# Graph network on one core: in the first edge stage the scatters wait for two copies at a time, the second following the first directly

## The chip, the cores and the metric

One Trainium2 chip, one of its cores. The time is the device time of one execution in microseconds (us); of several runs the median counts. A core has five engines that run side by side and meet by semaphores: TensorE (PE in the rows; PEld are its weight loads), VectorE (DVE), ScalarE (ACT), GpSimd (POOL) and SyncE (SP), which issues most DMAs. All DMAs are carried out by the core's 16 DMA engines. Indirect DMAs, whose rows are chosen by a list of indices, are issued by GpSimd.

## The reference, cut to what matters

A two-layer graph network on 12500 nodes of 160 features and 200000 edges, sorted by destination (`dst`), with random sources (`src`). The stage at hand is the message part of layer 0. Each edge takes the features of its `dst` node, mixes them with the edge's four attributes, and adds the message to its `src` node:

```
xj = node_features[col]                        # col = dst
m0 = s @ Wm_ss * dist * INV8 + einsum('eui,ei->eu', v, r_vec) @ Wm_vv * (...)
m1 = (s @ Wm_sv)[:, :, None] * r_vec[:, None, :] * INV8 + einsum('eui,uw->ewi', v, Wm_vs) * dist[:, :, None] * ...
msg = concatenate([m0, m1.reshape(e, 96)], axis=-1)
agg = segment_sum(msg, row, num_segments=n)    # row = src
```

The products with the weights are done per node in a stage before and stored in a table `T0`, so the edge stage gathers, scales and adds up. The sum over `u` of the vector parts is left as 32 partial sums, so a message has 192 numbers (`MSG0`). Layer 1, an attention layer, and the node updates follow in later stages.

## The kernel before, in words

The function `layer0_edges` (L328) runs through the edges in tiles of 128 (`R`), four tiles (`GT`) to a step, 392 steps in all, 8 steps (`STEPS`) to a pass of the loop (`passes`, L321). In a step, for each of its four tiles:

- SP loads the rows of `T0` that the tile needs (`e_win`, L389 and L390), three steps ahead. Once in four steps it loads also `e_local` (L377), `e_row` (L373, the tile's source nodes repeated over 128 partitions, 1024 KB), `e_at` (L369), and the data of a part of layer 1 that runs in this stage beside the edges (`r_xT` L682 in, `H` L690 out; class `Radial`).
- TensorE spreads the rows to the edges (L584), VectorE and ScalarE form the messages `u` (L476 to L486, L625). The edges of a tile may share a source node, and an accumulating scatter must not name a row twice; so TensorE multiplies the messages with the matrix `q` of equal sources (L597), which gives every edge the total of its node in this tile, and ranks.
- ScalarE copies the four tiles' totals from PSUM into one of four buffers (`e_total`, `evacuate`, L638). Ahead of that it waits until the scatters of the step four back, which read the same buffer, have landed.
- VectorE works out in `places` (L525 to L540) where each row goes: the first edge of a node in a tile to the node's row, all others to a dump row (`e_place`).
- GpSimd issues four indirect DMAs that add the rows to HBM (`sums`, L447), one per tile. Tile c of each step goes to its own copy of the sums, `sums[c]`; the four copies are added up in the next stage (`node_update0`). Since an accumulating DMA reads the sum and writes it later, the scatter into copy c must wait until the scatter of the step before into the same copy has landed. For this there are semaphores `added[p][c]`, by the parity p of the step and by the copy, which each scatter raises by 16.

The wait stands not at the scatter but at a tiny instruction ahead of it: `settle` (class `Settle`, L119) waits for its own last result and adds two zeros in one element (`e_pool_cell`, L129), and the scatter follows it in order on GpSimd. In a step's body, for c = 0 to 3: at c = 0 the waits for the buffer and the places (`total_ready`, `placed`); then the wait for `added[1 - p][c]`; then `settle`; then the scatter of copy c. `gate` (L113) is a wait that always holds.

Of the kernel before, what the change touches and what calls it, by code (L numbers as in the profile page):

```python
# [77 lines left out]
class Mem:  # L78
# [15 lines left out]
    def sem(self, name):  # L94
        self.sems.append(self.nc.alloc_semaphore(name))
        return self.sems[-1]
# [16 lines left out]
def gate(eng, k):  # L113


    eng.wait_ge(k["ready"], 4)
# [204 lines left out]
def passes(eng, body):  # L321
    body(0)
    with eng.Fori(1, PASSES - 1) as t:
        body(t)
    body(PASSES - 1)


def layer0_edges(nc, m, k, ps, W, T0, index, rows_src, LR, baseI, iota, attr, sums, es, H):  # L328
# [4 lines left out]
    with own:  # L333
# [15 lines left out]
        added = [[sem(f"e0_added{p}{c}") for c in range(GT)] for p in range(2)]  # L349
# [10 lines left out]
        settle = Settle(mm, k, "e0_pool")  # L360
# [4 lines left out]
        with nc.Block() as block:  # L365
# [66 lines left out]
            @block.gpsimd  # L432
            def _(pool):
                def body(t):
                    for r in range(STEPS):
                        i, p = At(t, r), r % 2
                        for c in range(GT):
                            if c == 0:
                                gate(pool, k)
                                pool.wait_ge(total_ready, i.n(1, 1))  # L440
                                gate(pool, k)
                                pool.wait_ge(placed, i.n(1, 1))
                            if not i.before(1):
                                gate(pool, k)
                                pool.wait_ge(added[1 - p][c], i.uses(64, 16 * ((r + 1) // 2)))
                            settle(pool, i.n(4, c))
                            pool.indirect_dma_start(sums[c], bass.IndirectOffsetOnAxis(ap=place[:, r % 4, c:c + 1], axis=0),  # L447
                                                    total[:, r % 4, c, 0:MSG0], None, compute_op=ALU.add
                                                    ).then_inc(added[p][c], 16)
                passes(pool, body)  # L450
                for p in range(2):
                    for c in range(GT):
                        pool.wait_ge(added[p][c], 16 * (SB // 2))
# [2518 lines left out]
```

## Time and profile before

| | us |
|---|---|
| median of 3 runs | 10577.76 |
| lowest, highest | 10567.25, 10608.22 |
| profiled execution | 10625.38 |
| its span | 10623.6 |

| engine | busy us | share of the span |
|---|---|---|
| PE | 8642.2 | 81% |
| DVE | 8012.2 | 75% |
| POOL | 7869.8 | 74% |
| PEld | 5524.9 | 52% |
| ACT | 4337.2 | 41% |

The shares are means over stages that are bound by different things. The first edge stage runs from about 487 to 3530 us of the span, so the views are to be read for this stretch. A row of the groups by line names the line, the engine, the operation, what it writes and reads, its count, the busy time in us and the mean time of one in ns, then the engine's idle time just before these instructions and what ended it. A row of the timeline has the start in us, the duration in us, engine, line and operation, and in brackets the idle time just before it. Of a DMA that GpSimd issues the row shows the time that GpSimd is busy with it, not the transfer. "issue" means that the engine waited for nothing that the profile shows.

### The profile page before, as it was taken

The numbers are of one execution on the slowest core, as the hardware profiler recorded it, in microseconds if no ns is written. First come the engines' busy times: TensorE is split into PE (matmuls) and PEld (weight loads), VectorE is DVE, ScalarE is ACT, GpSimd is POOL, SyncE is SP. The second block draws the span as 40 slices with busy tenths as digits, with TensorE's granted clock in tenths as the row PEclk, the third lists the DMA queues.
The fourth block names the chain that finished last, engine by engine and source line by source line (L and its number), as shares of the span: only waits on it lengthen the run. The fifth ranks groups of instructions, "written<-read, shape, count | busy, mean of one in ns | idle before, by whom it ended". The sixth has DMA issues, their size and how long they took to land. (4 is left out here: it accounts for less than half of the span.)

```text
span 10623.6 us, 176663 instructions
## 1 busy us (share of the span) xinstructions
PE 8642.2 (81%) x35512; PEld 5524.9 (52%) x35512; DVE 8012.2 (75%) x15399; ACT 4337.2 (41%) x7700; POOL 7869.8 (74%) x7782
## 2 busy tenths in 40 slices
PE   0888888888888799999996788777787878787588
PEld 0444444444444232222224777777777777777333
DVE  3277777777777588788886888888888888888565
ACT  0276666666666211111112333333333333333255
POOL 4488888888888777777775777777777777777332
PEclk9599999999999799999997989999899989899699
DMA  5588888888888999999993444444444444444222
GB/s 205 172 168 169 163 168 169 163 167 165 167 170 161 179 221 222 220 220 223 218 223 98 134 135 137 134 134 134 134 136 134 134 135 137 134 134 134 72 76 59
DMA packets 1202910, 1661.71 MB, mean 156 GB/s; under 512 B 215166, under 2 KB 814537, under 8 KB 1172553
## 3 DMA queue, kind: packets, MB, share of 16 engines
q1 hardware_dynamic: 806993, 1199.16, 42.2%
q0 software_dynamic: 395520, 458.93, 23.6%
q14 instruction: 353, 2.89, 0.1%
q8 instruction: 44, 0.72, 0.0%
HBM read 1483.21 MB, written 443.97 MB: 181 GB/s over the span
## 5 line engine op out<-in xcount | busy, mean ns | idle before, releaser
L447 POOL DMA_INDIRECT sums<-e_total,e_place x1568 | 2495.0, 1591 | 389.2 <-issue 223.0
L1847 POOL DMA_INDIRECT e_rows<-TD,e_at x1568 | 1613.6, 1029 | 477.6 <-issue 477.0
L1847 POOL DMA_INDIRECT e_rows<-TS,e_at x1568 | 1581.0, 1008 | 417.5 <-issue 330.5
L584 PE MATMUL ps<-e_win,e_pick 128*128 128x448 f32 x3136 | 1331.9, 570 | 165.2 <-DVE e_u L481 125.2
L2004 PE MATMUL ps<-w_r,e_h 128*128 128x224 f32 x3136 | 870.1, 432 | 518.4 <-DVE e_d L1889 470.5
L2108 ACT ACTIVATE e_dT<-ps 128x512 f32<-128x512 f32 x1176 | 671.7, 596 | 1185.7 <-PE ps L2016 1145.5
L584 PEld LDWEIGHTS ps<-e_win,e_pick 128*128 128x128 f32 x3136 | 614.7, 201 | 917.9 <-issue 833.1
L1098 POOL TENSOR_TENSOR n_zv<-n_zv,n_ast 128x1536 f32<-128x1536 f32 x200 | 730.8, 3654 | 467.6 <-DMA n_zv<-in_x_columns 456.9
L129 POOL TENSOR_TENSOR e_pool_cell<-zeros 1x1 f32<-1x1 f32 x1568 | 939.4, 599 | 87.5 <-DVE e_place L540 59.1
L2004 PEld LDWEIGHTS ps<-w_r,e_h 128*128 128x128 f32 x3136 | 675.8, 227 | 593.3 <-DVE e_d L1889 485.5
L2040 PE MATMUL ps<-w_lb,e_dT 128*128 128x192 f32 x3136 | 836.3, 348 | 4.6 <-issue 3.8
L1278 PE MATMUL ps<-n_z,w_uss 128*64 128x512 f32 x1600 | 745.1, 609 | 24.5 <-DVE n_z L1121 23.9
L2016 PE MATMUL ps<-ident,e_d 128*128 128x128 f32 x4704 | 743.2, 302 | 6.6 <-issue 4.2
L747 DVE SCALAR_TENSOR_TENSOR r_y<-ps,w_rb,r_rstd 128x512 f32<-128x512 f32 x394 | 295.5, 750 | 586.5 <-issue 516.2
L1102 POOL TENSOR_TENSOR n_zv<-n_zv 128x512 f32<-128x512 f32 x400 | 695.0, 1737 | 36.9 <-POOL n_zv L1102 0.4
L2016 PEld LDWEIGHTS ps<-ident,e_d 128*128 128x128 f32 x4704 | 661.7, 160 | 47.6 <-issue 7.9
L2028 PE MATMUL ps<-e_val,e_q 128*128 128x168 f32 x3136 | 642.0, 329 | 53.2 <-ACT e_tot L2119 19.1
L2041 PE MATMUL ps<-w_la,e_dT 128*128 128x160 f32 x3136 | 681.8, 299 | 0.0
L716 PE MATMUL ps<-r_sq,w_avg 128*128 128x512 f32 x788 | 446.9, 651 | 277.7 <-issue 277.7
L597 PEld LDWEIGHTS ps<-e_u,e_q 128*128 128x128 f32 x3136 | 541.7, 192 | 187.9 <-issue 187.9
L597 PE MATMUL ps<-e_u,e_q 128*128 128x194 f32 x3136 | 586.3, 330 | 0.0
L1859 DVE TENSOR_TENSOR e_m<-e_rows 128x640 f32<-128x640 f32 x392 | 321.7, 821 | 341.5 <-DMA e_rows<-TD,e_at 192.8
(433 smaller groups left out, 19205.2 us busy)
## 6 DMA issues: line engine op xcount, KB each, us to landing
e_win<-T SPq DMA_DIRECT2D x1568, 168.0 KB
n_z<-in_x_columns SPq DMA_DIRECT2D x400, 512.0 KB
n_zv<-in_x_columns SPq DMA_DIRECT2D x800, 192.0 KB
TOT<-e_tot SPq DMA_DIRECT2D x392, 352.0 KB
e_row<-in_src_rows SPq DMA_DIRECT2D x98, 1024.0 KB
e_row<-in_dst_rows SPq DMA_DIRECT2D x98, 1024.0 KB
e_win<-T SPq DMA_DIRECT2D x1568, 56.0 KB
e_local<-LR SPq DMA_DIRECT2D x98, 512.0 KB
```

The source lines that it names most:

```text
L129: pool.tensor_tensor(self.cell[:], z, z, ALU.add).then_inc(self.done, 1)
L447: pool.indirect_dma_start(sums[c], bass.IndirectOffsetOnAxis(ap=place[:, r % 4, c:c + 1], axis=0), total[:, r % 4, c, 0:MSG0], None, compu ...
L584: pe.matmul(g[:, c, :], pick[:, p, R * c:R * c + R], win[:, s, c, :], start=True, stop=True).then_inc(spread, 1)
L597: last = pe.matmul(out[:, c, :], q[:, p, c, :], u[:, p, c, :], start=True, stop=True)
L1098: pool.tensor_tensor(zv[:, b], zv[:, b], ast[:, g.p], ALU.mult).then_inc(zv_ready, 1)
L1102: pool.tensor_tensor(zv[:, b, 0], zv[:, b, 0], zv[:, b, i], ALU.add).then_inc(zv_ready, 1)
L1278: last = pe.matmul(ps[0:S, U0, :], W["uss"][:, 4 * s + j, :], z[:, s % 4, j, :], start=False, stop=False)
L1847: pool.indirect_dma_start(rows[:, p, x, c, :], None, table, bass.IndirectOffsetOnAxis(ap=at[:, gp, x, col:col + 1], axis=0)).then_inc(rows ...
L2004: last = pe.matmul(w4[:, c, 0:224], hh[:, p, R * c:R * c + R], W["r3"][:], start=True, stop=True)
L2016: last = pe.transpose(ps[:, bank(i, j), R * c:R * c + R], d[:, p, c, j, :], I[0:R, 0:R])
L2040: pe.matmul(head(c)[:, :, 0:24], dT[:, 1, e], W["lb"][:].rearrange("u h x -> u (h x)"), start=True, stop=False)
L2041: pe.matmul(head(c)[:, :, 0:20], dT[:, 0, e], W["la"][:].rearrange("u h x -> u (h x)"), start=False, stop=True)
```

## The change

The four scatters of a step form two pairs. Ahead of c = 0 GpSimd waits for the landings of the step before into copies 0 and 1, then there is one `settle`, and the scatters of copies 0 and 1 follow one another with nothing between; the same for copies 2 and 3. So there are two `settle` a step where there were four, and the scatters of copies 1 and 3 have their wait one scatter earlier. What is transferred stays the same.

```
-                            if not i.before(1):
-                                gate(pool, k)
-                                pool.wait_ge(added[1 - p][c], i.uses(64, 16 * ((r + 1) // 2)))
-                            settle(pool, i.n(4, c))
+                            if c % 2 == 0:
+                                for also in range(c, c + 2):
+                                    if not i.before(1):
+                                        gate(pool, k)
+                                        pool.wait_ge(added[1 - p][also], i.uses(64, 16 * ((r + 1) // 2)))
+                                settle(pool, i.n(2, c // 2))
                             pool.indirect_dma_start(sums[c], bass.IndirectOffsetOnAxis(ap=place[:, r % 4, c:c + 1], axis=0),
                                                     total[:, r % 4, c, 0:MSG0], None, compute_op=ALU.add
                                                     ).then_inc(added[p][c], 16)
```

## Rows read from the trace of the kernel before

**Rows 1.** Busy us (and instructions) per engine of one stretch, clock, DMA share, GB/s.

```profile
core 0: us, PE busy (x) PEld busy (x) DVE busy (x) ACT busy (x) POOL busy (x), PEclk, DMA share, GB/s
2000.00:2300.00 300.00, 254.32 (x775) 139.45 (x775) 214.08 (x485) 201.39 (x333) 257.82 (x312) 0.97 0.83 168
```

**Rows 2.** Groups by line, GpSimd, 480 to 3560 us.

```profile
L447 POOL DMA_INDIRECT sums<-e_total,e_place x1568 | 2495.0, 1591 | 389.2 <-issue 223.0 <-DMA sums<-e_total,e_place 152.1 <-POOL e_pool_cell L129 14.0
...
L129 POOL TENSOR_TENSOR e_pool_cell<-zeros 1x1 f32<-1x1 f32 x1568 | 939.4, 599 | 87.5 <-DVE e_place L540 59.1 <-DMA sums<-e_total,e_place 18.0 <-issue 10.1
```

**Rows 3.** Timeline of GpSimd: a step with e_row and the next one's start.

```profile
2008.14 2.04 POOL L447 DMA_INDIRECT sums<-e_total,e_place  x1 [0.24 <-DMA sums<-e_total,e_place]
...
2010.48 1.55 POOL L447 DMA_INDIRECT sums<-e_total,e_place  x1 [0.24 <-issue]
2011.49 0.61 POOL L129 TENSOR_TENSOR e_pool_cell<-zeros 1x1 f32<-1x1 f32 x1
2012.34 1.55 POOL L447 DMA_INDIRECT sums<-e_total,e_place  x1 [0.24 <-issue]
...
2014.20 1.55 POOL L447 DMA_INDIRECT sums<-e_total,e_place  x1 [0.24 <-issue]
2015.63 0.19 POOL L129 TENSOR_TENSOR e_pool_cell<-zeros 1x1 f32<-1x1 f32 x1
2016.28 1.55 POOL L447 DMA_INDIRECT sums<-e_total,e_place  x1 [0.46 <-DMA sums<-e_total,e_place]
```

**Rows 4.** Waits, 480 to 3560 us: waiting line, releaser: us in total, times, longest.

```profile
ACT e_total L638 <- DMA sums<-e_total,e_place: 368.0, 258, 3.3
...
POOL e_pool_cell L129 <- DMA sums<-e_total,e_place: 18.0, 22, 2.0
```

**Rows 5.** Timeline of ScalarE: its copies into the buffers (three of them).

```profile
2018.20 0.82 ACT L638 ACTIVATE e_total<-ps 128x776 f32<-128x776 f32 x1 [1.49 <-DMA sums<-e_total,e_place]
...
2035.17 0.82 ACT L638 ACTIVATE e_total<-ps 128x776 f32<-128x776 f32 x1 [1.04 <-DMA sums<-e_total,e_place]
...
2049.68 0.82 ACT L638 ACTIVATE e_total<-ps 128x776 f32<-128x776 f32 x1 [0.63 <-PE ps L597]
```

**Rows 6.** Timeline of GpSimd: plain scatters of an earlier stage, directly following.

```profile
300.18 0.96 POOL L833 DMA_INDIRECT T<-n_out,place_rank  x1 [1.31 <-DVE n_out L822]
301.44 0.96 POOL L833 DMA_INDIRECT T<-n_out,place_rank  x1 [0.30 <-issue]
```

**Rows 7.** Timeline of GpSimd: gathers of the second edge stage.

```profile
6008.48 0.95 POOL L1847 DMA_INDIRECT e_rows<-TD,e_at  x1 [0.30 <-issue]
6009.73 0.94 POOL L1847 DMA_INDIRECT e_rows<-TD,e_at  x1 [0.30 <-issue]
6010.68 0.18 POOL L129 TENSOR_TENSOR e_gather_cell<-zeros 1x1 f32<-1x1 f32 x1
6011.02 1.24 POOL L1847 DMA_INDIRECT e_rows<-TS,e_at  x1
```

**Rows 8.** Timeline of GpSimd: the stage's last scatter.

```profile
3521.40 1.55 POOL L447 DMA_INDIRECT sums<-e_total,e_place  x1 [0.24 <-DMA sums<-e_total,e_place]
```

**Rows 9.** Timeline of GpSimd: the next group of four steps, in parts.

```profile
2029.62 1.64 POOL L447 DMA_INDIRECT sums<-e_total,e_place  x1 [0.24 <-DMA sums<-e_total,e_place]
...
2033.43 1.55 POOL L447 DMA_INDIRECT sums<-e_total,e_place  x1 [0.24 <-issue]
...
2035.29 1.55 POOL L447 DMA_INDIRECT sums<-e_total,e_place  x1 [0.24 <-DMA sums<-e_total,e_place]
...
2039.01 2.01 POOL L447 DMA_INDIRECT sums<-e_total,e_place  x1 [0.24 <-issue]
...
2046.58 0.18 POOL L129 TENSOR_TENSOR e_pool_cell<-zeros 1x1 f32<-1x1 f32 x1
2047.25 1.55 POOL L447 DMA_INDIRECT sums<-e_total,e_place  x1 [0.48 <-DMA sums<-e_total,e_place]
```

**Rows 10.** Timeline of SyncE's queue: issues of the two big loads.

```profile
2029.46 0.35 SPq L377 DMA_DIRECT2D e_local<-LR  x1
...
2040.12 0.34 SPq L373 DMA_DIRECT2D e_row<-in_src_rows  x1
```

## The prediction

> **What bounds the kernel now.** I read the table of stretches first, then the groups by line, then the timelines. In the first edge stage (some 487 to 3530 us; 392 steps, 98 groups of four) no engine is saturated by its average: in a stretch of 300 us GpSimd is busy 257.8 us, TensorE 254.3, VectorE 214.1, and the DMA engines 0.83 of the time [rows 1]. The groups show 1568 scatters of 1591 ns and 1568 small additions of 599 ns on GpSimd [rows 2]. The sum of both is no load to be halved: the timeline shows that they overlap. A scatter starts at 2010.48 and ends 1.55 later at 2012.03; the small addition starts at 2011.49, inside it, and ends at 2012.10; the next scatter starts at 2012.34 [rows 3]. So the pitch is 1.86 us per scatter, 7.44 per step of four; 392 steps of 7.44 are 2916 us of a stage of some 3030.
>
> That GpSimd, and nothing else, sets the stage is seen on ScalarE. Its copy of a step's sums into one of the four buffers waits for the scatters of the step four back. It sat idle for that 258 times, 368.0 us in all, while the small additions sat idle for a landing only 22 times, 18.0 us [rows 4]. At 2018.20 the copy starts because a scatter has landed [rows 5]; a scatter started after 2014.20 would have had 1.92 us, so it is that of 2014.20, the last of its step (copy 3). Then the starts at 2008.14 and 2016.28 are copies 0 of two steps [rows 3]. GpSimd begins step i+1 at 2016.28 while ScalarE fills the buffer of step i+4: work is queued nearly three steps deep. Whatever GpSimd gains or loses per step, the stage gains or loses, until something else is late.
>
> **Removed: two small additions per step, 784 in all.** Each shows 599 ns [rows 2], which would be 470 us, but what matters is when the next scatter could start without it. Elsewhere GpSimd issues transfers directly one behind another: a plain scatter starts at 300.18, takes 0.96, and the next starts at 301.44, idle 0.30 [rows 6]. A gather at 6008.48 takes 0.95 and the next starts at 6009.73, again 0.30. With a small addition between them (6009.73, took 0.94; addition 6010.68; next 6011.02) it is 0.35 [rows 7]. Behind an accumulating scatter with its addition it is 0.31 (2012.03 to 2012.34, rows 3). So 0.30 after the end of the one before is what a transfer needs with nothing between, and the addition lies in the shadow of it. Is the scatter itself longer for the addition? The stage's last one, with none behind it, also shows 1.55 [rows 8]. I take the saving as 0.01 us each: 784 x 0.01 = 8 us, which I count as zero. The ends of the range: zero, and 0.55, if the next scatter could start 0.30 after the point where the addition now starts (1.01 after the start; 1.31 instead of 1.86). No row shows two accumulating scatters directly following; the direct rows all say 0.30 after the end, so I stay at that end.
>
> **Added: an earlier wait for half of the copies.** Copy 1 of a step used to wait for its own predecessor only just ahead of itself, four pitches (7.44 us) after that one's start. Now copy 0 waits for both, three pitches (5.58) after the start of the old copy 1; copy 2 likewise for the old copy 3. Queued behind the waiting addition are both scatters of the pair and all that follows on GpSimd; who waits for those is ScalarE's copy four steps on, so with GpSimd the bound the wait is paid in full. How late may a landing be? Where an addition starts late (2015.63), the scatter starts 0.65 behind it (2016.28), with the addition itself 0.19 [rows 3]. So a landing costs nothing up to 5.58 - 0.65 = 4.93 us after its scatter's start; under the old code it was 7.44 - 0.65 = 6.79. I take the landing as the time when the waiting instruction starts, which is a little late by itself.
>
> Landings from rows: copy 3 of 2014.20 by 2018.20: 4.00 us, inside 4.93 [rows 3, 5]. But copy 3 of 2029.62 by 2035.17: 5.55 [rows 5, 9]; the load of e_local was issued at 2029.46 [rows 10]. Copy 0 of 2008.14 by the late addition at 2015.63: 7.49 [rows 3], copy 0 of 2039.01 by 2046.58: 7.57 [rows 9]; that is the step in which e_row is loaded (issue 2040.12, rows 10). These big loads come once in four steps, so a group of four has two quiet steps and two with late landings. The group then pays:
> Step with e_row: its copy 0 waits for copy 1 of the step before, started at 2033.43 behind the same loads. With the 5.55 of the copy 3 two scatters earlier it lands at 2038.98, and copy 0 starts at 2039.63 instead of 2039.01 [rows 9]: 0.62 us. The latency is a neighbour's, so this is an estimate.
> Step after it: copy 0 already waits for the old copy 0 (2015.63) and would now wait for copy 1, too. That one landed between 2015.63 and the 2018.20 of copy 3 [rows 3, 5]; evenly spaced, a third of 2.57, 0.86 later. In the next group it is between 2046.58 and 2049.68 [rows 5, 9]: a third of 3.10, 1.03, an upper value since that copy to the buffer was not released by the scatter.
> Sometimes a third: copy 2 at 2035.29 would have had to wait for the 2035.17 of the old copy 3: 2035.82, 0.53 late [rows 5, 9]. But it delays the very scatters that the first term delays, so I don't add it.
> Sum: 0.62 + 0.86 = 1.48, with the second group 0.62 + 1.03 = 1.65; I take 1.5 us. The first four steps and the last pay nothing, so 96 groups: 96 x 1.5 = 144 us. Bounds: only the term with the measured wait, 96 x 0.62 = 60 us; the old copy 1 landing with copy 3, 96 x (0.62 + 2.57) = 306 us.
>
> The four gates and four waits for landings per step stay on GpSimd's queue, only earlier; SP's and VectorE's queues hold nothing that is changed. The later stages start later by what this one loses and are otherwise as before.
>
> The profiled execution took 10625.38 us (span 10623.6), 47.6 above the median of the runs, 10577.76. The change as a difference: 10625.4 + 144 = 10769 for a profiled one, and **10722 us** against the median.
>
> **Rivals.**
> Rival 1, faster: a scatter that directly follows starts before the first has ended. For it: the addition is accepted 1.01 us after the scatter's start, 0.54 before its end, which the addition behind a gather (6009.73, 6010.68) is not [rows 3, 7]. Against it: every direct pair shown waits for the end, and the late addition's own 0.65 shows that something more than the addition stands ahead of a scatter. Price: 0.55 x 2 x 392 = 431 us gained; the allowed landing shrinks from 4.93 to 4.38, so the two waits per group grow by 0.55 each: 96 x (1.5 + 1.1) = 250 us. Net 181 faster, 10397 us, under the cap of the 368 us that ScalarE waits [rows 4]. It decides from 144 / 784 = 0.18 us saved per pair; below that the change loses.
> The Trainium skill, Perfetto Trace Analysis, section "DMA Instruction — SWDGE (GPSIMD)", says that the end shown is where the last of two processors has written its last descriptor, each executing from a queue of its own; by that the first processor might run ahead, yet the last still sets the pitch, and the sum would stay. No row here separates the two.
> Rival 2, no change: landings come earlier once GpSimd pauses, because a late landing is mostly the wait behind other scatters. Then the old copy 1 lands within 4.93, little is paid, and the time is 10578 to 10620. For it: several scatters are in flight at a latency of 4 to 7.5 and a pitch of 1.86 [rows 3, 5]. Against it: the quiet steps have the same pitch and land in 4.00, so the large loads make the difference, and those stay.
> The Trainium skill, DMA: Bandwidth & Descriptors, section "Anatomy of one DMA — SWDGE (gpsimd) path", gives about 2.0 us plus bytes / 436e3; an estimate from it for the 98 KB of a copy is 2.2 us, by which no landing would be late and rival 2's time would come out. The 4.00 us of rows 3 and 5 is well above it, so the measured value stands.
> Rival 3, slower still: the old copy 1 lands nearly with copy 3, up to the 306 us above: 10884.
>
> **Chances.** Forecast 0.67, rival 1 0.15, rival 2 0.14, rival 3 0.04. A measurement of this kernel tells about 0.5% (53 us) from no change. Faster by more is rival 1, 0.15; within it is rival 2, 0.14; slower is the forecast and rival 3, 0.71. The range reaches from rival 2's side, 10560, where a few hundredths saved per pair would also put it, to 10840, near twice the forecast's loss; it leaves out rival 1 and most of rival 3. The forecast's own range is 10640 to 10840 (60 us to some 260).
>
> **What would show it.** In the changed profile: the second scatter of a pair starts 1.85 to 1.86 us after the first (forecast) or 1.31 (rival 1). The small additions number 784; in the steps with and behind e_row they start late, followed by the scatter at 0.65, and the small additions' idle time put down to landings rises well above 18.0 us. ScalarE's wait for landings grows by about as much as the stage. The stage lasts some 3175 us. Wrong would be: a pitch below 1.7 inside pairs; or late additions as rare as now.

## The result and the profile after

The changed kernel took 10700.35 us (median of 4 runs, 10696.18 to 10712.84), the kernel before 10591.21 beside it (4 runs, 10567.25 to 10608.22): 1.010 of its time, 95% interval 1.0084 to 1.0116, 109 us slower. The forecast of 10722 had 144 us more than before. The profiled execution has a span of 10710.9 us.

Groups by line, GpSimd, 480 to 3700 us, of the changed kernel (line, engine, operation, count | busy us, mean ns | idle us before them and what ended it), to set against [rows 2]:

```profile
L449 POOL DMA_INDIRECT sums<-e_total,e_place x1568 | 2470.5, 1576 | 478.2 <-issue 360.9 <-DMA sums<-e_total,e_place 114.6 <-ACT e_total L640 2.7
L129 POOL TENSOR_TENSOR e_pool_cell<-zeros 1x1 f32<-1x1 f32 x784 | 386.0, 492 | 151.2 <-DMA sums<-e_total,e_place 90.9 <-DVE e_place L542 56.5 <-issue 1.3
```

The waits, same stretch (waiting line, releaser: us in total, times, longest), against [rows 4], and below them the scatters' row in the view of the tile `sums` (shortest, median and longest in ns, start of the first and the last), first of the kernel before, then of the changed one:

```profile
ACT e_total L640 <- DMA sums<-e_total,e_place: 503.3, 279, 4.5
...
POOL e_pool_cell L129 <- DMA sums<-e_total,e_place: 90.9, 143, 3.2
```

```profile
L447 POOL DMA_INDIRECT sums<-e_total,e_place x1568: 1552/1553/2083, 496.4 to 3521.4; - x196
```

```profile
L449 POOL DMA_INDIRECT sums<-e_total,e_place x1568: 1541/1553/2078, 494.0 to 3618.1; - x196
```

784 small additions are gone, and the scatters of the stage still take 3124.1 us from first to last start where they took 3025.0: 99.1 us more, nearly all of the 109. The stage is slower by what GpSimd waits. The additions' idle time until a landing rose from 18.0 us (22 times) to 90.9 (143 times), and ScalarE's from 368.0 to 503.3: it waits for what GpSimd issues later.

Timeline of GpSimd in the changed kernel, one group of four steps in part, and after it SyncE's issues of the big transfers in the same stretch:

```profile
2012.34 1.55 POOL L449 DMA_INDIRECT sums<-e_total,e_place  x1 [0.24 <-issue]
2014.20 1.54 POOL L449 DMA_INDIRECT sums<-e_total,e_place  x1 [0.31 <-DMA sums<-e_total,e_place]
...
2017.97 1.63 POOL L449 DMA_INDIRECT sums<-e_total,e_place  x1 [0.30 <-DMA sums<-e_total,e_place]
2019.06 0.60 POOL L129 TENSOR_TENSOR e_pool_cell<-zeros 1x1 f32<-1x1 f32 x1
2019.91 1.55 POOL L449 DMA_INDIRECT sums<-e_total,e_place  x1 [0.25 <-issue]
2021.77 1.54 POOL L449 DMA_INDIRECT sums<-e_total,e_place  x1 [0.30 <-issue]
2024.21 0.18 POOL L129 TENSOR_TENSOR e_pool_cell<-zeros 1x1 f32<-1x1 f32 x1 [0.91 <-DMA sums<-e_total,e_place]
2024.86 1.55 POOL L449 DMA_INDIRECT sums<-e_total,e_place  x1 [0.47 <-issue]
...
2034.15 1.93 POOL L449 DMA_INDIRECT sums<-e_total,e_place  x1 [0.30 <-issue]
2037.75 0.18 POOL L129 TENSOR_TENSOR e_pool_cell<-zeros 1x1 f32<-1x1 f32 x1 [1.68 <-DMA sums<-e_total,e_place]
2038.41 1.55 POOL L449 DMA_INDIRECT sums<-e_total,e_place  x1 [0.48 <-issue]
```

```profile
2017.81 0.35 SPq L377 DMA_DIRECT2D e_local<-LR  x1
2020.65 0.91 SPq L692 DMA_DIRECT2D H<-r_h  x2
2021.85 1.18 SPq L684 DMA_DIRECT2D r_xT<-in_edge_attr  x2
2029.08 0.34 SPq L373 DMA_DIRECT2D e_row<-in_src_rows  x1
```

Two things are to be read. First, the pair at 2012.34 and 2014.20: 1.55 busy, 0.31 idle, next scatter, with no addition between; with one between it was 0.31 as well [rows 3]. The addition was in the shadow. Over the whole stage the median distance from the first scatter of a pair to its second is 1.858 us, and from there to the second pair of the step 1.854, where both were 1.860: 0.008 us less per addition dropped, 6 us in all. Second, two late additions. The scatter of 2021.77 ends at 2023.31, the next could start 0.30 later at 2023.61 and starts at 2024.86: its addition, at 2024.21, waited for the landing of the scatter of 2017.97 (copy 3 of the step before, three pitches ahead of it; its landing released the addition 6.2 us after its start, with e_local, H and r_xT issued beside it). And 2038.41 comes 2.03 us after the 2036.38 at which it could have started, in the wake of e_row.

To see where the waits stand in all groups, I took the start of each of the 1568 scatters in the timeline, less the end of the one before it, less 0.306, from step 10 on, and summed by the position of the step in its group of four and by the copy. Position 2 is the step beside which H and r_xT are issued (e_local at the end of the step ahead of it), position 3 that of e_row. Only these places hold more than 8 us in either kernel:

```
us ahead of            before   changed
copy 0 of position 3      0.1      67.1
copy 0 of position 0     23.0      59.7
copy 2 of position 2      0.1      31.3
all places               40.2     168.1
scatters over 1.553 us   58.8      33.8     (the issue itself)
```

So 128 us of waits were added, and 25 us came back because the scatters' own issue is shorter (mean 1576 instead of 1591 ns): net 103 us, against 99.1 from first to last scatter and 109 in all. Of the 25 us some 7 are the 0.01 us by which a second scatter of a pair is shorter (1.54 instead of 1.55); the rest is fewer long issues (of the 392 scatters of copy 0, 56 took more than 1.6 us, now 10).

The landings themselves can be read too: each scatter's semaphore is updated 16 times, and the trace has the times (all 16 for 1374 of the 1528 scatters from step 10 on in the kernel before, for 1469 in the changed one). From a scatter's start to the last update that is recorded, mean over the stage:

```
us                                 before   changed
copy 3 of position 1                 4.92      4.95
copy 1 of position 2                 5.49      5.64
copy 1 of position 3                 5.79      5.26
all scatters                         4.46      4.33
```

The first three are the ones that copy 2 of position 2, copy 0 of position 3 and copy 0 of position 0 wait for since the change. Of the 186 waits of over 0.15 us whose landings are complete in the changed trace, every one ended with the landing of the pair's second copy, whose scatter started three pitches before; the addition started 0.24 us after the landing and the scatter 0.89 (medians). So the allowance is 5.58 - 0.89 = 4.69 us by this clock, which is the prediction's 4.93 by the start of the addition.

### The profile page after: what moved, and what is told of

Read it like the earlier page. It is cut to its first block and busy times, and to the rows that moved or that the text cites. A ratio compares the mean times of both kernels' runs of the same rounds, so it can differ in the third digit from the quotient of the medians.

```text
span 10710.9 us, 175127 instructions
## 1 busy us (share of the span) xinstructions
PE 8672.5 (81%) x35512; PEld 5531.8 (52%) x35512; DVE 8008.2 (75%) x15399; ACT 4328.3 (40%) x7700; POOL 7814.8 (73%) x6998
## 5 line engine op out<-in xcount | busy, mean ns | idle before, releaser
L449 POOL DMA_INDIRECT sums<-e_total,e_place x1568 | 2470.5, 1576 | 478.2 <-issue 360.9
L586 PE MATMUL ps<-e_win,e_pick 128*128 128x448 f32 x3136 | 1357.6, 579 | 184.0 <-DVE e_u L483 144.0
L2030 PEld LDWEIGHTS ps<-e_val,e_q 128*128 128x128 f32 x3136 | 493.0, 202 | 149.3 <-ACT e_tot L2121 127.2
```

Of the source, the lines that this page charges most:

```text
L586: pe.matmul(g[:, c, :], pick[:, p, R * c:R * c + R], win[:, s, c, :], start=True, stop=True).then_inc(spread, 1)
L2030: last = pe.matmul(tot2[:, c % 2], q[:, j % 2, c, :], val[:, slot // 4, 4 * (slot % 4) + c, :], start=True, stop=True)
```

## The experiments

The experiments ran on three further chips. On that of e1, e3, e4 and e5 the kernel before took 12215.66 us, on that of e2, e9, e10 and e11 12620.63 (the stages behind this one are longer there), on that of e7, e12, e13 and e14 10621.6. So I compare ratios to the kernel before on the same chip, and the scatters' first-to-last time within the stage. There is no profile of the kernel before on these chips, so a stage's length is compared across chips with care. The places of waits are worked out as above.

**Early waits, four additions (e1).** Each scatter keeps its addition, only the waits move.

```
                            if c % 2 == 0:
                                for also in range(c, c + 2):
                                    ...
                                        pool.wait_ge(added[1 - p][also], ...)
                            settle(pool, i.n(4, c))
```

> The earlier waits alone: ahead of copy 0 GpSimd waits for copies 0 and 1, ahead of copy 2 for copies 2 and 3, but each of the four scatters keeps its small addition. Theory A (the additions lie in the shadow of the 0.30 us that a transfer needs after the one before, and the earlier waits are the whole loss): as the changed kernel, 10700 us within 10, ratio 1.010. Theory B (dropping 784 additions did save up to 0.24 us each, and the waits cost 109 us plus that): slower than the changed kernel by up to 188 us, 10890.

Measured: 1.0114 (1.0079 to 1.0150). **The changed kernel again (e2)**, for comparison:

> The changed kernel once more, beside the next two on one chip, since the chip of the runs so far took some 15% longer in later stages. Both theories: 1.009 to 1.012 of the kernel before, the first edge stage about 3120 us between first and last scatter, where the earlier waits with four additions had 3160. If dropping the additions saves what that difference says, 40 us, Theory B is not quite dead; if the stage comes out at 3150 to 3160 here, it was the chip.

Measured: 1.0126 (1.0091 to 1.0161). In the view of the tile `sums`, first e1, then e2:

```profile
L449 POOL DMA_INDIRECT sums<-e_total,e_place x1568: 1552/1553/2074, 501.9 to 3662.4; - x196
```

```profile
L449 POOL DMA_INDIRECT sums<-e_total,e_place x1568: 1542/1553/2093, 498.3 to 3649.0; - x196
```

3160.5 and 3150.7 us, each on its chip. The earlier waits alone bring the whole loss, and theory B falls: by it e1 would have been up to 188 us slower than the changed kernel, and the ratios differ by no more than their intervals. The 10 us between the two stages don't measure the additions, since the same changed kernel took 27 us longer in e2 than in its first profile (3124.1). What the additions are worth is seen from the distances above, 0.01 us each.

**Two additions ahead of each scatter (e5)**, in the kernel before.

```
                            settle(pool, i.n(8, 2 * c))
                            settle(pool, i.n(8, 2 * c + 1))
```

> The kernel before with two small additions ahead of each scatter instead of one, the second waiting for the first. It measures how much cover they have. Theory A: the first ends 0.07 us after the scatter before it, the second cannot; with 0.65 from a late addition's start to the scatter's it would add about 0.4 us x 1568 = 630 us, with 0.15 from its end, as behind a gather, about 0.14 x 1568 = 220 us: 10810 to 11220. Theory E (additions run beside the scatters' issue whatever their number): no change, 10591.

Measured: 1.0248 (1.0209 to 1.0288), 303 us. Timeline of GpSimd in this kernel:

```profile
2001.11 1.55 POOL L448 DMA_INDIRECT sums<-e_total,e_place  x1 [0.16 <-issue]
2002.13 0.86 POOL L129 TENSOR_TENSOR e_pool_cell<-zeros 1x1 f32<-1x1 f32 x2
2003.15 1.55 POOL L448 DMA_INDIRECT sums<-e_total,e_place  x1 [0.16 <-issue]
```

The pitch is 2.04 instead of 1.86: the second addition costs its 0.18. It ends 0.33 after the scatter before it (2002.99 and 2002.66), and the next starts 0.16 later, 0.49 after the scatter's end instead of 0.31. With one addition, which ends 0.07 after the scatter, 0.07 and 0.16 fit into these 0.31. So the cover is some 0.30 us wide and a second addition doesn't fit. Of theory A only the smaller figure was of the right kind (220 us forecast); the 0.65 of a late addition doesn't apply here, so it belongs to an addition that was waited for, not to any that ends after the scatter. Theory E falls.

**Only the first pair (e3).** Copies 2 and 3 keep their own wait and addition.

```
                            if c != 1:
                                for also in ((0, 1), (), (2,), (3,))[c]:
                                    ...
                                settle(pool, i.n(3, max(0, c - 1)))
```

> Only copies 0 and 1 form a pair; copies 2 and 3 keep their own waits and additions. Theory A: the loss splits by where GpSimd stands idle in the changed kernel, some three quarters of it ahead of copy 0, so about 80 of 109 us stay: 10670. Theory C (each pair costs alike): half, 10645. Theory D (only one pair is needed to bring all of the loss, since a delay at copy 0 gives the other waits time): 10700.

Measured: 1.0088 (1.0058 to 1.0119), against 1.0114 of e1 on this chip. The interval holds both A and D, and C lies just below it, so the ratio doesn't decide. The places of the waits tell more: ahead of copy 2 of position 2 there are 0.6 us (42.5 in e1), ahead of copy 0 of position 3 there are 94.4 (58.9 in e1), ahead of copy 0 of position 0 54.2 (79.1), and in all 159.7 of 192.7. Less the 40.2 us that the kernel before has, 78% of e1's added waits are left, near the three quarters of theory A in size. But the reason that A gave for it, that each wait stands for itself, is only half of it: copies 2 and 3 wait 47 us less, mostly at position 2, and copy 0 of the next step, position 3, waits 35 us more, copy 0 of position 0 after it 25 us less. A wait that is taken away comes back in part at the next one, as theory D had it, but D's "all of the loss" doesn't hold.

**All four scatters behind one wait (e4).**

```
                            if c == 0:
                                for also in range(GT):
                                    ...
                                settle(pool, i.n(1))
```

> One wait for all four copies and one addition a step, four scatters directly following. The landing of copy 3 is then waited for right after its start. Theory A (a step lasts three pitches of 1.86, the landing of copy 3, and 0.65): 5.58 + 4.0 + 0.65 = 10.2 us instead of 7.72, 392 steps: about 970 us more, 11560, between 11450 and 11700; the landing stays near 3.5 to 4 us even with nothing else in flight, and the pitch inside the four is 1.86. Theory F (landings are long because scatters queue behind one another, and fall towards 2 us when they are few): about 8.4 us a step, 10870.

Measured once: 13450.01 against 12215.66, 1234 us more, above the range that both theories gave. Timeline of GpSimd in this kernel, two steps:

```profile
2002.04 1.55 POOL L449 DMA_INDIRECT sums<-e_total,e_place  x1 [0.47 <-issue]
2003.89 1.54 POOL L449 DMA_INDIRECT sums<-e_total,e_place  x1 [0.31 <-issue]
2005.74 1.54 POOL L449 DMA_INDIRECT sums<-e_total,e_place  x1 [0.30 <-issue]
2007.59 1.54 POOL L449 DMA_INDIRECT sums<-e_total,e_place  x1 [0.30 <-issue]
2012.39 0.18 POOL L129 TENSOR_TENSOR e_pool_cell<-zeros 1x1 f32<-1x1 f32 x1 [3.27 <-DMA sums<-e_total,e_place]
2013.04 1.57 POOL L449 DMA_INDIRECT sums<-e_total,e_place  x1 [0.47 <-issue]
...
2018.62 1.54 POOL L449 DMA_INDIRECT sums<-e_total,e_place  x1 [0.30 <-DMA sums<-e_total,e_place]
2022.44 0.18 POOL L129 TENSOR_TENSOR e_pool_cell<-zeros 1x1 f32<-1x1 f32 x1 [2.27 <-DMA sums<-e_total,e_place]
```

The form is theory A's: three pitches of 1.85 (2002.04 to 2007.59), the landing of copy 3, then 0.65. The landing, 4.80 and 3.82 us here until its addition starts, was set too low with 4.0: from 496.5 to 4760.6 (first and last start) a step takes 10.91, which leaves 10.91 - 5.55 - 0.65 = 4.7. GpSimd pauses for some 3 us in each step (additions' idle time 1276.5 us in all), and the landings don't fall towards 2 us: by the semaphores the shortest with all 16 updates took 3.40 us, and the median is 3.60, where it was 3.93 in the kernel before on another chip. Theory F falls.

**Pairs with eight tables (e7).** Even and odd steps add to tables of their own; the next stage adds up four of them.

```
                                        pool.wait_ge(added[p][also], i.uses(64, 16 * (r // 2)))
                                ...
                            pool.indirect_dma_start(sums[GT * p + c], ...
```

> The changed kernel, pairs and two additions per step, but odd and even steps add to different tables, eight in all, so that a pair waits for landings of two steps back (13 us allowed instead of 4.93). The next stage adds up four of the eight only, and the other four are not cleared: the sum of the odd steps is left out. Theory A (the whole loss is the earlier wait): the small additions hardly ever wait for a landing (under 10 us in all), the pitch stays 1.86, and the kernel is at or a little under the kernel before, 0.993 to 0.999. Theory G (two scatters directly following disturb something else, or the landings delay ScalarE's copy): 1.005 or more.

Measured: 0.9942 (0.9923 to 0.9961), within theory A's range. Groups by line and the view of the tile, of this kernel:

```profile
L449 POOL DMA_INDIRECT sums<-e_total,e_place x1568 | 2492.6, 1590 | 433.4 <-issue 417.7 <-DMA sums<-e_total,e_place 11.1 <-POOL e_pool_cell L129 4.4
L129 POOL TENSOR_TENSOR e_pool_cell<-zeros 1x1 f32<-1x1 f32 x784 | 470.8, 600 | 66.3 <-DVE e_place L542 61.4 <-issue 4.5
```

```profile
L449 POOL DMA_INDIRECT sums<-e_total,e_place x1568: 1541/1553/2080, 497.0 to 3479.8; - x196
```

No addition waits for a landing; the waits of all places are 3.8 us, and the scatters take 2982.8 from first to last. With the pairs as they are in the changed kernel, the loss is gone: it is the wait and nothing else of the pair. Nor have the landings become shorter by the other tables: their mean is 4.63 us here, 4.46 in the kernel before; they are only allowed more. The kernel is 60 us under the kernel before, and its stage 42 us under that of the profile before on another chip, about the waits which that one had (40.2). The version isn't a faster kernel, for it leaves four tables out of the sum; clearing and adding them up wasn't tried.

**What makes the landings late.** First, the big loads spread over the steps, in the kernel before (e10) and in the changed one (e11):

```
-                        if r % 4 == 3 and not final:
...
-                            load_row(r // 4, t + 1)
+                            load_row(r // 4, 0, t + 1)
+                        if r in (4, 5, 6) and not final:
+                            load_row(0, r - 3, t + 1)
+                        if r in (0, 1, 2) and not i.before(8):
+                            load_row(1, r + 1, t)
```

and `load_local` in the same way; H is stored at r % 4 == 3.

> The kernel before, with the big loads of the first edge stage spread: e_row and e_local come in four quarters, one in each step, each quarter with its own semaphore, and the results H are stored a step later than the next r_xT is loaded. The same bytes. Theory L (large loads beside the scatters make landings late): little to gain here, since the old waits allow 6.8 us: the late small additions and the longer issues (2.04 instead of 1.55) go, some 30 to 60 us faster, ratio 0.994 to 0.997. Theory Q (landings are late because scatters queue behind one another): no change.

> The changed kernel with the same spread loads. Theory L: landings stay under 4.93 us in nearly all steps, so the waits for pairs cost nothing any more: within 0.3% of the kernel before with spread loads, so 0.994 to 1.000 of the kernel before, and the small additions' idle time for landings falls from 90.9 us to under 30. Theory Q: the loss stays, 1.010.

Measured: e10 0.9978 (0.9951 to 1.0004), a little above theory L's range and not told apart from no change, and e11 1.0118 (1.0086 to 1.0150), which theory L excluded. The additions' wait in e11:

```profile
POOL e_pool_cell L129 <- DMA sums<-e_total,e_place: 116.3, 128, 3.0
```

It was 101.0 in e2 on this chip. **Only e_row spread (e9)**, in the changed kernel:

> The changed kernel with e_row alone spread over four steps; e_local, H and r_xT as they were. Theory L, by what my prediction said (the wait after the step with e_row is the larger, 0.86 of 1.48 us): more than half of the loss goes, ratio 1.004. By what the changed kernel's timeline seems to say (the larger wait comes after the step with e_local, H and r_xT): most of the loss stays, 1.007 to 1.010.

Measured: 1.0096 (1.0064 to 1.0129). Most of the loss stays, as the changed kernel's timeline said and the prediction's split of it did not. Then, on another chip, **r_xT nearly left out**, in the changed kernel (e13) and the one before (e14), both with spread loads, and **r_xT in two halves (e12)**:

```
-            sp.dma_start(self.xT[:, p, :], self.es[bass.ds(2 * t + p, 1)]...
+            sp.dma_start(self.xT[:, p, 0:wide], self.es[bass.ds(2 * t + p, 1), :, 0:wide]...
```

> The changed kernel with spread loads and r_xT loaded in full only once; after that each of its loads brings 16 of 512 columns, so the part of layer 1 that runs in this stage works on stale inputs (left out: 504 of 512 KB of loads per four steps). In the run with spread loads the late landings were left in the step in which r_xT is loaded. Theory L (large reads beside the scatters make them land late): the small additions' idle time for landings falls from 116.3 to under 40 us and the kernel comes to 0.992 to 0.998 of the kernel before. Theory Q (the scatters' own queue, or the pair's wait itself, makes them late): the idle time stays above 90 us, ratio above 1.008.

> The same left out of the kernel before with spread loads: the base for the run above. Theory L: 0.990 to 0.995 of the kernel before, the pitch of 1.86 us in nearly every scatter; the difference to the changed kernel without these loads under 0.4%. Theory Q: the difference stays 1.4%.

> The changed kernel with spread loads and the two halves of r_xT loaded in two steps, 256 KB each instead of 512 KB at once; all bytes kept. Theory L: the loss falls by about a half, idle for landings 40 to 80 us, ratio 1.003 to 1.008. Theory Q: 1.012 as with 512 KB.

Measured: e13 1.0065 (1.0044 to 1.0086), e14 0.9941 (0.9920 to 0.9963), e12 1.0107 (1.0085 to 1.0128). The additions' wait in e13:

```profile
POOL e_pool_cell L129 <- DMA sums<-e_total,e_place: 69.0, 109, 1.5
```

In e12 it was 112.1. The pair costs 1.0065 / 0.9941, 1.2% with r_xT left out, and 1.0118 / 0.9978, 1.4%, with it; the intervals don't tell these apart. So as a forecast of the time theory L failed three times (e11, e13, e12); for e13 theory Q failed too. But the places of the waits follow the loads:

```
us ahead of            e2: as    e9: e_row   e11: spread,   e12: as e11,     e13: as e11,
                       changed   spread      H a step on    r_xT in halves   r_xT left out
copy 0 of position 0     85.1        3.2         12.0           96.4             73.4
copy 0 of position 3     55.4       45.8         55.4           22.2              6.5
copy 2 of position 2     38.0      123.1         68.1           31.8              9.1
copy 2 of position 1      0.6        4.5         11.9           34.6             33.9
all places              187.2      189.1        186.0          216.4            149.4
```

Spreading e_row empties the place behind it (85.1 to 3.2). Leaving r_xT out nearly empties the two places beside it (6.5 and 9.1, where e12 on the same chip has 22.2 and 31.8, and e11 on another 55.4 and 68.1). Each time other places hold the waits, and the sum hardly falls (189, 186), or by a third with nearly half a megabyte of loads per group left out (149 against 216 in e12). Theory Q as I wrote it doesn't hold either: with a pause in each step the landings of e4 still take 4.08 us on average by the semaphores, where it was 4.46 in the kernel before.

The landings themselves show what keeps the sum up. On the chip of e7, e12, e13 and e14 almost all of them can be read. Of the scatters of copies 1 and 3, for which the pairs wait, 12% land later than 6 us with the loads as they are (e7), 5% with the loads spread (e12); but later than the allowed 4.69 us land 39% in e7, 44% in e12, and still 38 and 35% in e14 and e13, with r_xT left out. The median landing of all scatters is 4.12 us in e7 and 4.48, 4.42 and 4.24 in e12, e14 and e13. So spreading the loads made very late landings rarer and ordinary ones later, and as many as before are over the allowance. The kernels compared differ in their tables and additions as well, so this is a reading of four traces, not an experiment; why the ordinary landing grows isn't shown.

## Why the prediction was right

- **GpSimd's pitch as the bound.** Right: waits of 128 us more and issues of 25 us less make 103 us, where the stage grew by 99 and the kernel by 109.
- **Removing an addition saves nothing.** Right: 1.86 inside a pair, seen in 2012.34 and 2014.20 and in the medians, and e1 against e2. Rival 1, which needed 0.18 us per pair, had 0.01. Where the argument took the 0.30 between transfers of other stages over to accumulating scatters, it held.
- **Added wait.** Right in kind. The late additions of the changed kernel start 0.24 us after the landing of the second copy, and the scatter follows at 0.65: the threshold (three pitches less 0.65) is as told, and e7, which changes the allowance and with it only the tables, takes the loss away.
- **The sum.** 144 us against 109; by terms, per group of four (98 groups, the tables above). First term, copy 0 of the step with e_row: 0.62 expected, 67.1 / 98 = 0.68 measured, and together with the third wait that the prediction let go into it, 31.3 / 98 = 0.32, it is 1.00. Second term, copy 0 of the step after: 0.86 on top of the old wait expected, (59.7 - 23.0) / 98 = 0.37 measured. This is the term that was too large, and not because its landing was guessed: the prediction set copy 1 of the step with e_row at 6.01 us (2016.49 less 2010.48), and in the kernel before the semaphores give 5.79 plus the 0.24 until an addition starts, 6.03. What it held fixed was the landing itself. In the changed kernel it comes at 5.26, half a microsecond sooner. The load of e_row is also issued earlier beside it (median 0.03 us after the start of copy 0, before 1.09); whether that or GpSimd's pause brings it isn't shown. Last, the shorter issues, -25.0 / 98 = -0.26, of which the prediction had 0.08 as the 8 us that it counted as zero. The first term too small and the issues left out nearly cancel, which is luck, so the sum is off by about the second term.
- **Rival 2** had its share of truth in the second term and in the 25 us: one late landing came sooner. But landings didn't fall under 4.93 in general; their mean went from 4.46 us to 4.33. The estimate of 2.2 us from the Trainium skill, DMA: Bandwidth & Descriptors, section "Anatomy of one DMA — SWDGE (gpsimd) path", is not what these scatters show: no landing with all 16 updates took less than 3.40 us in the kernel before, nor in e4, where GpSimd pauses in each step.
- **What I named as its proof** came as told: 784 additions, late ones followed by the scatter at 0.65 (2024.21 and 2024.86; 2037.75 and 2038.41). ScalarE's wait rose by 135 us, somewhat more than the stage. The stage was forecast at 3175 and came to about 3130.

## What to carry to other kernels

An instruction's removal is worth what it lets start earlier, so compare the gap in front of the next transfer with and without it, in any stage that has such a pair, before counting its busy time. A merged wait takes over the age of its youngest transfer, here three pitches instead of four; where the waiting engine is the bound, the tail of late landings is then paid in full. And an added wait moves everything behind it, the transfers that it waits for included: a landing time read before the change need not hold after it. Where waits stand in a chain on one engine, taking away one of them or its cause gave only a part back here; allowing every landing more time (another set of tables) gave back all.

## What the runs showed of the hardware

- An accumulating scatter of 128 rows of 768 bytes takes GpSimd 1.55 us, or 1.54 when it directly follows another; the next transfer starts 0.30 after its end. A one-element addition between them costs 0.01 us at most, a second 0.18 (e5).
- A scatter's landing took 3.40 us at the least after its start, 3.93 in the median and 4.46 on average in the kernel before; with H, r_xT or e_row issued beside it 5.1 to 6.4 on average (copy 0 of positions 2 and 3). A waiting addition starts 0.24 us after the landing, and the scatter behind it 0.65 later. Issues of up to 2.08 us instead of 1.55 occur beside big loads (2.04 at 2008.14 and 2.01 at 2039.01, rows 3 and 9), and there were fewer of them where GpSimd waited (58.8 us over the usual in the kernel before, 33.8 in the changed one).
- The same programs took 15 to 19% longer on two of the chips (12215.66 and 12620.63 us against 10591.21), by the stages after the first edge stage; in the changed kernel this stage took 3150.7 us on the second of them against 3124.1. From 6000 to 10000 us of the span the granted TensorE clock was 0.78 in e2 and 0.90 to 0.91 in the first profile of the changed kernel. What slowed these stages isn't shown.
